# Two block scales rewritten as tensor_scalars, two convolution taps put beside a pair of state sums, and every slot chosen anew

## The chip, the core and the metric

The kernel runs on one core of a Trainium2 chip. A core has a matrix engine (TensorE, PE in the profile), a vector engine (VectorE, DVE), a scalar engine (ScalarE, ACT), a general engine (GpSimd, POOL), and SyncE (SP), which issues most of the DMAs here. Each engine takes its own instructions in order, and the engines wait for each other by semaphores. The metric is the device time of one execution in microseconds, lower is better. The kernel before takes 4279.77 us (median of 3 runs, 4276.45 to 4279.84).

## The reference

The input is x of shape (16, 1024, 256). Two blocks follow each other, both with a residual:

```
x = x + mamba(layernorm(x))
x = x + fp4_ffn(layernorm(x))

mamba:   xz = h @ in_proj.T;  x, z = split(xz)              # 512 channels each, 4 heads of 128
         x = silu(conv_b + sum_k xpad[:, k:k+L] * w[:, k])  # causal, 4 taps
         B, C, dt = per head projections of x (16 states)
         delta = softplus(dt @ dtw + dt_b)
         s = s * exp(delta * A) + (delta * x) * B           # for each of 16 states, over time
         y = (sum_n s_n * C_n + x * D) * silu(z);  out = y @ out_proj.T

fp4_quant_dequant(v): in blocks of 16 elements
         scale = max(max|v| / 6, 1e-12)
         q = nearest of (0, .5, 1, 1.5, 2, 3, 4, 6) to |v/scale|, with sign, times scale
ffn:     h = silu(q(v) @ q(w_gate).T) * (q(v) @ q(w_up).T);  out = q(h) @ q(w_down).T   # 256 -> 704 -> 256
```

## The kernel before

A *unit* is one head and one chunk of 512 time steps: 16 sequences, 2 chunks, 4 heads, so 128 units. There are also 128 *tiles* of 128 tokens for the normalisations and the feed-forward block, so one unit and one tile fall on the same stretch of time. A unit has 16 *steps*, one for each state n. In the second chunk of a sequence (a *late* unit) the scan starts from a carried value; in the first (an *early* unit) it starts from zero.

The scan runs on VectorE: in each step one `tensor_tensor_scan` over 512 columns (L990, tile `state`), and for twelve of the sixteen states also a product of the broadcast B row with delta*u in PSUM (L969, tile `db`). For the other four states GpSimd makes that product (`drive`, L739, tile `brow`). TensorE spreads a row of B over the partitions (`spread_b`, L1038), ScalarE makes exp(delta*A) (`decay_of`, L481). GpSimd multiplies two states at a time with C (`weigh`, L748, tile `prod`), and TensorE adds such a pair up (`sum_up`, L1053). It does that in quarters of its array: 64 rows by 64 columns each, the states of the pair into `ybank` and, crossed over, into `cross`. At the end `cross` is copied out, turned by `swap` and added to `ybank` (L1160), and VectorE multiplies with silu(z) (tile `yg`, L952).

Around the scan lie the jobs of the other stages. `timetable` gives each of them a slot: `due("post", 46)` is true in the step whose number is 46 modulo 16, in the unit that is 46 // 16 units behind the job's start. A job's slot number on an engine sets where it stands in that engine's order, and within a step the order of the `if` lines decides. On VectorE three places in a step take jobs: the product for the next step, `between`, the scan, and `behind`.

The jobs that the change and the prediction touch, with the lines of the profile:

- Block scales of the activations. VectorE takes the largest magnitude of each block of 16 (L831: 16 blocks of v in 256 columns, 44 blocks of h in 704 columns), then the scale (`block_scale`, L834), then its reciprocal (`block_recip`, L839). `block_scale` is a `scalar_tensor_tensor` with two inputs in SBUF: the maxima, and a one-column tile `least` that holds 1e-12, read again for each column. GpSimd then multiplies v (L803) or h (L780) by the reciprocals, and after the rounding by the scales (L788, L765).
- Rounding. ScalarE writes magnitudes to PSUM (L558 for v, L630 and L646 for the halves of h), VectorE adds and subtracts (`step_up`, L893, and `step_down`, L896). For h these are called `round_up_h` and `round_down_h`.
- The gate. TensorE makes the gate (L1108) and up (L1075) products in two halves of 352 columns, ScalarE the silu (L498), VectorE their product (`gated`, L903).
- The convolution. TensorE adds four taps into `pbank`: tap 0 in two diagonal quarters beside the D term (L1225, L1228), taps 1 to 3 as whole 128 by 128 products (`conv_tap`, L1061).
- delta. TensorE subtracts rounded pieces (L1281, L1168) and makes the dt product (L1156); ScalarE takes pieces (L580) and the softplus (L641) between two table loads (L638, L643).

All products in f32 come out as two instructions each in the trace.

## Time and profile before

| | |
|---|---|
| median of 3 runs | 4279.77 us |
| profiled execution | 4271.48 us |
| its span | 4269.6 us |
| busy: VectorE | 4170.9 us, 98% |
| busy: TensorE | 3979.2 us, 93% |
| busy: GpSimd | 3792.8 us, 89% |
| busy: ScalarE | 3697.7 us, 87% |
| first and last scan start | 87.7 and 4178.6 us |

Busy is the union of an engine's instructions over the span. On VectorE an instruction's record begins before the one ahead of it has ended, so what an instruction costs the engine is the distance from its start to the start of the next, some 0.07 to 0.1 us under its own duration. A short wait can hide in that overlap and does not show as idle time. Most of the span is one steady stretch in which units follow each other; in the first 90 us the weights are quantised, and in the last 90 us only the feed-forward of the last tiles is left.

### The profile page before, as it was taken

To read this page: it belongs to the slowest core of one execution; us is meant where nothing else is said; L and a number is where in the kernel's file an instruction comes from. 1 tells how busy PE (TensorE), PEld (TensorE's weight loads), DVE (VectorE), ACT (ScalarE), POOL (GpSimd) and SP (SyncE) were. 2 spreads that over 40 slices of the span, in tenths; PEclk is the share of its full clock that TensorE was granted. 3 is DMA by queue.
4 is the path that set the end of the run, shared out by engine and by line. 5 is a ranking of instruction groups with operands and counts; after the bars stand their busy time and mean duration, and the time that the engine had idled before them with its cause. 6 is when DMAs were issued, how large, how long until landed. Compare 5 with 4: busy or idle time off the path is not lost. (4 is left out here: it accounts for less than half of the span.)

```text
span 4269.6 us, 66216 instructions
## 1 busy us (share of the span) xinstructions
PE 3979.2 (93%) x19184; PEld 1930.0 (45%) x19500; DVE 4170.9 (98%) x5812; ACT 3697.7 (87%) x6808; POOL 3792.8 (89%) x2334
## 2 busy tenths in 40 slices
PE   4889999999999999999999999999999999999988
PEld 1234444444444444444444444444444444444445
DVE  6999999999999999999999999999999999999995
ACT  4889899898888889888888888989888888988874
POOL 5889999999999999999899999999999999999984
PEclk8999999999999999999999999999999999999999
DMA  3655555555555555555555555555555555555551
GB/s 98 199 178 184 176 177 182 178 177 181 179 175 181 181 172 183 179 172 181 176 174 181 181 175 178 183 177 177 180 180 176 178 182 172 182 180 174 180 172 33
DMA packets 288974, 739.16 MB, mean 173 GB/s; under 512 B 35686, under 2 KB 87014, under 8 KB 288614
## 3 DMA queue, kind: packets, MB, share of 16 engines
q1 hardware_dynamic: 286912, 732.75, 53.1%
q8 instruction: 159, 2.61, 0.2%
q10 hardware_dynamic: 1702, 2.16, 0.2%
q14 instruction: 201, 1.65, 0.1%
HBM read 709.61 MB, written 25.17 MB: 172 GB/s over the span
## 5 line engine op out<-in xcount | busy, mean ns | idle before, releaser
L748 POOL TENSOR_TENSOR prod<-state,cs 128x1024 f32<-128x1024 f32 x1024 | 2401.7, 2362 | 5.3 <-PE cross L1053 2.9
L1053 PE MATMUL ybank<-prod,ident 64*64 64x512 f32 x4096 | 997.0, 604 | 75.9 <-DVE state L990 55.7
L969 DVE TENSOR_TENSOR db<-db,du 128x512 f32<-128x512 f32 x1536 | 1046.2, 681 | 13.7 <-remote 7.3
L481 ACT ACTIVATE decay<-delta,aneg 128x512 f32<-128x512 f32 x1536 | 1029.4, 711 | 0.1
L1053 PE MATMUL cross<-prod,ident 64*64 64x512 f32 x4096 | 996.8, 605 | 0.0
L990 DVE TENSOR_TENSOR_SCAN state<-decay,carry,db 128x512 f32<-128x512 f32 x768 | 956.1, 1259 | 0.0
L990 DVE TENSOR_TENSOR_SCAN state<-decay,db 128x512 f32<-128x512 f32 x768 | 911.4, 1201 | 8.6 <-PE bank_b L1313 8.6
L739 POOL TENSOR_TENSOR brow<-brow,du 128x512 f32<-128x512 f32 x512 | 653.1, 1276 | 153.2 <-DMA brow<-b_rows 152.9
L1038 PE MATMUL db<-pieces,sel 128*128 128x512 bf16 x1220 | 468.0, 384 | 89.6 <-DVE state L990 88.4
L1053 PEld LDWEIGHTS ybank<-prod,ident 64*64 64x64 f32 x4096 | 239.8, 132 | 523.6 <-issue 386.6
L481 ACT ACTIVATE db<-delta,aneg 128x512 f32<-128x512 f32 x512 | 352.5, 688 | 137.3 <-DVE state L990 136.2
L1123 PE MATMUL bank_a<-wd,ht 128*128 128x256 f32 x1536 | 406.4, 389 | 4.3 <-ACT ht L506 1.2
L1038 PEld LDWEIGHTS db<-pieces,sel 128*128 128x128 bf16 x1536 | 149.4, 97 | 550.9 <-DVE state L990 354.2
L1123 PEld LDWEIGHTS bank_a<-wd,ht 128*128 128x128 f32 x1536 | 283.8, 191 | 205.2 <-issue 178.0
L1075 PE MATMUL bank_b<-wu,vt 128*128 128x352 f32 x1024 | 357.3, 471 | 0.0
L1108 PE MATMUL bank_a<-wg,vt 128*128 128x352 f32 x1024 | 347.5, 462 | 2.0 <-ACT hh L498 2.0
L990 DVE TENSOR_TENSOR_SCAN state<-db,carry,brow 128x512 f32<-128x512 f32 x256 | 325.5, 1272 | 0.0
L990 DVE TENSOR_TENSOR_SCAN state<-db,brow 128x512 f32<-128x512 f32 x256 | 310.1, 1211 | 0.0
L1075 PEld LDWEIGHTS bank_b<-wu,vt 128*128 128x128 f32 x1024 | 184.0, 189 | 215.5 <-issue 159.0
L1149 PE MATMUL pbank<-xnt,win 128*128 128x512 f32 x512 | 264.1, 601 | 2.3 <-ACT delta L641 1.8
L1138 PE MATMUL bank_a<-wo,yg 128*128 128x256 f32 x1024 | 265.2, 383 | 0.0
L1149 PE MATMUL bank_a<-xnt,win 128*128 128x512 f32 x512 | 262.5, 594 | 0.0
(140 smaller groups left out, 7240.6 us busy)
## 6 DMA issues: line engine op xcount, KB each, us to landing
cs<-c_rows SPq DMA_DIRECT2D x1024, 512.0 KB, 3.8
brow<-b_rows SPq DMA_DIRECT2D x512, 256.0 KB, 4.3
xin<-in_hidden SPq DMA_DIRECT2D x128, 128.0 KB, 4.5
xres<-in_hidden SPq DMA_DIRECT2D x128, 128.0 KB, 4.4
out_x<-ot SPq DMA_DIRECT2D x128, 128.0 KB, 3.4
c_rows<-xdbl SPq DMA_DIRECT2D x128, 32.0 KB, 2.1
b_rows<-xdbl SPq DMA_DIRECT2D x128, 32.0 KB, 2.0
win<-in_win_t SPq DMA_DIRECT2D x1, 1024.0 KB, 5.2
```

What stands on the lines that cost most here:

```text
L481: act.activation(out, delta[:, w.mod(2), :], ACT.Exp, scale=aneg[:, w.mod(HEADS), n:n + 1]).then_inc(done, 1)
L739: pool.tensor_tensor(brow[:, s, :], brow[:, s, :], du[:, w.mod(2), :], ALU.mult).then_inc(db_pool, 1)
L748: pool.tensor_tensor(prod[:, r, :, :], state[:, 2 * p:2 * p + 2, :], cs[:, c, :, :], ALU.mult).then_inc(weighted, 1)
L969: dve.tensor_tensor(t[:, :], t[:, :], du[:, gu % 2, :], ALU.mult).then_inc(db_done, 1)
L990: dve.tensor_tensor_scan(state[:, n, :], by, plus, start, ALU.mult, ALU.add).then_inc(scanned, 1)
L1038: pe.matmul(db[g % DB_BANKS][:, :], sel[:, gn, :], pieces[:, gu % 2, :], start=True, stop=True).then_inc(b_spread, 1)
L1053: last = pe.matmul((ybank, cross)[k][c * Q:(c + 1) * Q, :], ident[rows, rows], prod[rows, p % P_RING, k, :], start=(p == 0), stop=(k == 1 ...
L1075: last = pe.matmul(bank_b[:, 0:HALF], vt[:, k, :], wu[:, k, part * HALF:(part + 1) * HALF], start=(k == 0), stop=(k == KM - 1))
L1108: last = pe.matmul(bank_a[:, 0:HALF], vt[:, k, :], wg[:, k, part * HALF:(part + 1) * HALF], start=(k == 0), stop=(k == KM - 1))
L1123: last = pe.matmul(bank_a[:, 0:DM], ht[:, k, :], wd[:, k, :], start=(k == 0), stop=(k == KI - 1))
L1138: last = pe.matmul(bank_a[:, 0:DM], yg[:, t.mod(8) // 4, h, i * P:(i + 1) * P], wo[:, h, :], start=(h == 0), stop=(h == HEADS - 1))
L1149: return pe.matmul((pbank, bank_a)[part][:, :], win[:, k, part * DI + h * P:part * DI + (h + 1) * P], xnt[:, v.mod(8) // 4, k, :], start=( ...
```

## The change

1. `block_scale` is a `tensor_scalar` with two immediates (1/6 and 1e-12) in place of the `scalar_tensor_tensor`; the tile `least` is gone. For v, the maxima stand in a tile of their own and are read three times over (a dimension of step 0), and 48 columns are written in one run, of which the first 16 are used. For h, the maxima are written as 11 rows of 4 in a tile with 5 columns a row, and the scale reads these 11 rows of 4 and writes 44 columns in one run. The reciprocals move to other rows of the same tiles.
2. `taps_beside`: taps 1 and 2 of the convolution are computed as two diagonal quarters each (the matrix of a tap is diagonal, so the other two quarters are zero), and each quarter stands beside a crossed quarter of pair 1 of the state sums. Both states of pair 1 go into `cross`; `ybank` gets nothing of this pair. Tap 3 and the other seven pairs are as before.
3. All slots and the order of the `if` lines within a step are different on every engine, `between` is empty, and the buffer waits stay the same in kind.

```diff
-                return dve.scalar_tensor_tensor(s[:, 1, :], s[:, 0, :], 1.0 / 6.0,
-                                                least[0:s.shape[0], :].broadcast_to([s.shape[0], s.shape[2]]),
-                                                ALU.mult, ALU.max)
+                return dve.tensor_scalar(s[:, 1, :], s[:, 0, :], 1.0 / 6.0, SCALE_MIN, ALU.mult, ALU.max)
...
+            def v_scales():
+                three = v_max[:, None, :].broadcast_to([P, 3, DM // BLK])
+                return dve.tensor_scalar(vs[:, 0:3, :], three, 1.0 / 6.0, SCALE_MIN, ALU.mult, ALU.max)
+
+            def h_maxima(h):
+                return dve.tensor_reduce(h_max[:, :, 0:H_LONG], h.rearrange("p (a b k) -> p a b k", a=H_ROWS, k=BLK),
+                                         AX, ALU.max, apply_absolute_value=True)
+
+            def h_scales():
+                return dve.tensor_scalar(hs[:, 0, :].rearrange("p (a b) -> p a b", a=H_ROWS), h_max[:, :, 0:H_LONG],
+                                         1.0 / 6.0, SCALE_MIN, ALU.mult, ALU.max)
...
+            def taps_beside(v, w, p):
+
+                if v:
+                    x = xearly if v.mod(PER) < HEADS else xlate
+                if w:
+                    pe.wait_ge(weighted, w.val(PAIRS, p + 1))
+                for i in range(2):
+                    for r in range(2):
+                        rows, others = slice(r * Q, (r + 1) * Q), slice((1 - r) * Q, (2 - r) * Q)
+                        if v:
+                            pe.matmul(pbank[rows, :], cdiag[rows, v.mod(HEADS), i + 1, rows], x[rows, i + 1:i + 1 + CH],
+                                      start=False, stop=False, tile_position=(r * Q, r * Q), skip_group_check=True)
+                        if w:
+                            last = pe.matmul(cross[others, :], ident[rows, rows], prod[rows, p % P_RING, i, :],
+                                             start=False, stop=False, tile_position=(r * Q, (1 - r) * Q),
+                                             skip_group_check=True)
+                if w:
+                    last.then_inc(summed, 1)
...
-                if t := due("post", 36):
-                    gated(t, 0)
+                if t := due("post", 37):
+                    gated(t, 0)
```

Three places of the new order. First VectorE, in the middle of a late unit: the second half of a tile's quantisation work. `vs` and `hh` are the scales of v and the tile of h, `hw` the scratch of the rounding, `yg` the unit's gated output; a scan is listed as a SCALAR_TENSOR_TENSOR into `state`. Before:

```order
L903 TENSOR_TENSOR hh<-hh,bank_b 128x352
L969 TENSOR_TENSOR db<-db,du 128x512
L990 SCALAR_TENSOR_TENSOR state<-db,carry,brow 128x512
L893 SCALAR_TENSOR_TENSOR hw<-cross,hh 128x352
L831 TENSOR_REDUCE vs<-v_eps 128x16
L896 SCALAR_TENSOR_TENSOR hh<-cross,hw 128x352
L969 TENSOR_TENSOR db<-db,du 128x512
L990 SCALAR_TENSOR_TENSOR state<-decay,carry,db 128x512
L834 SCALAR_TENSOR_TENSOR vs<-vs,least 128x16
L952 TENSOR_TENSOR yg<-ybank,sz 128x512
L839 RECIPROCAL vs<-vs 128x16
L893 SCALAR_TENSOR_TENSOR hw<-cross,hh 128x352
```

Now the same work reads:

```order
L1004 SCALAR_TENSOR_TENSOR state<-db,carry,brow 128x512
L908 TENSOR_TENSOR hh<-hh,bank_b 128x352
L931 TENSOR_REDUCE v_max<-v_eps 128x16
L898 SCALAR_TENSOR_TENSOR hw<-cross,hh 128x352
L844 TENSOR_SCALAR vs<-v_max 128x48
L983 TENSOR_TENSOR db<-db,du 128x512
L1004 SCALAR_TENSOR_TENSOR state<-decay,carry,db 128x512
L901 SCALAR_TENSOR_TENSOR hh<-cross,hw 128x352
L921 RECIPROCAL vs<-vs 128x16
L983 TENSOR_TENSOR db<-db,du 128x512
L1004 SCALAR_TENSOR_TENSOR state<-decay,carry,db 128x512
L898 SCALAR_TENSOR_TENSOR hw<-cross,hh 128x352
```

The first `gated` (L903, now L908) moved behind the scan of the step whose `db` product used to follow it. The second rounding of h (the last row of each) moved behind one more product and scan, and `yg` moved from ahead of it to behind it.

Second TensorE, at the taps. `cdiag` holds the taps' diagonals, `win` the input projection, `sel` the selector for a row of B. Before:

```order
L1225 MATMUL pbank<-xearly,cdiag 64x512
L1228 MATMUL cross<-uu,ddiag 64x512
L1038 MATMUL db<-pieces,sel 128x512
L1149 MATMUL bank_a<-xnt,win 128x512
L1038 MATMUL db<-pieces,sel 128x512
L1237 MATMUL bank_b<-ident,v_eps 128x128 x2
L1061 MATMUL pbank<-xearly,cdiag 128x512 x3
L1149 MATMUL bank_a<-xnt,win 128x512
```

Now, from the last of the four rows of `taps_beside` on:

```order
L1090 MATMUL pbank<-xearly,cdiag 64x512
L1093 MATMUL cross<-prod,ident 64x512
L1067 MATMUL ybank<-prod,ident 64x512 x2
L1067 MATMUL cross<-prod,ident 64x512 x2
L1182 MATMUL bank_a<-xnt,win 128x512
L1052 MATMUL db<-pieces,sel 128x512
L1208 MATMUL bank_b<-ident,v_eps 128x128 x2
L1075 MATMUL pbank<-xearly,cdiag 128x512
L1052 MATMUL db<-pieces,sel 128x512
L1182 MATMUL bank_a<-xnt,win 128x512
```

The first two rows stand four times in a row in a unit; one whole tap is left of three, and pair 2 (the two rows at L1067) has come up to this place.

Third TensorE, around the up and gate products that ScalarE and VectorE wait for (`wu`, `wg`; `less` belongs to the pieces of B, `dtws` to delta, `swap` to the end of the sum). Before:

```order
L1075 MATMUL bank_b<-wu,vt 128x352 x2
L1038 MATMUL db<-pieces,sel 128x512
L1168 MATMUL pbank<-mid,less 128x512
L1108 MATMUL bank_a<-wg,vt 128x352 x2
L1038 MATMUL db<-pieces,sel 128x512
L1156 MATMUL pbank<-xdbl,dtws 128x512
L1160 MATMUL ybank<-xlate,swap 128x512
L1075 MATMUL bank_b<-wu,vt 128x352 x2
```

Now (up is L1108 here and gate L1141):

```order
L1052 MATMUL db<-pieces,sel 128x512
L1197 MATMUL pbank<-mid,less 128x512
L1108 MATMUL bank_b<-wu,vt 128x352 x2
L1141 MATMUL bank_a<-wg,vt 128x352 x2
L1052 MATMUL db<-pieces,sel 128x512
L1288 MATMUL pbank<-xdbl,dtws 128x512
L1052 MATMUL db<-pieces,sel 128x512
L1108 MATMUL bank_b<-wu,vt 128x352 x2
```

A selector product and the subtraction of pieces now stand ahead of the first up product; the product with `swap` moved behind the second one.

## Rows read from the trace of the kernel before

**Rows 1.** The page, part 1: busy us, share of the span, instructions.

```profile
PE 3979.2 (93%) x19184; PEld 1930.0 (45%) x19500; DVE 4170.9 (98%) x5812; ACT 3697.7 (87%) x6808; POOL 3792.8 (89%) x2334
```

**Rows 2.** Busy by stretch: stretch, its us; PE, PEld, DVE, ACT, POOL; clock, DMA, GB/s.

```profile
300.00:800.00 500.00, 476.18 (x2324) 231.06 (x2362) 499.23 (x703) 446.85 (x826) 456.81 (x282) 1.00 0.55 176
```

**Rows 3.** Waits of VectorE, whole span: us in total, times, longest.

```profile
DVE ot L939 <- PE bank_a L1123: 13.9, 8, 8.6
```

**Rows 4.** The same view, all there is between 500 and 4000 us.

```profile
DVE hh L903 <- PE bank_b L1075: 0.2, 1, 0.2
```

**Rows 5.** Line 834, the block scales: ns least/median/most, first and last start.

```profile
L834 DVE SCALAR_TENSOR_TENSOR vs<-vs,least x128: 141/160/744, 236.7 to 4237.0; 128x16 f32<-128x16 f32 x128
L834 DVE SCALAR_TENSOR_TENSOR hs<-hs,least x128: 189/389/2364, 282.4 to 4252.7; 128x44 f32<-128x44 f32 x128
```

**Rows 6.** Timeline of VectorE: start us, us, line, operation.

```profile
2020.08 2.33 DVE L834 SCALAR_TENSOR_TENSOR hs<-hs,least 128x44 f32<-128x44 f32 x1
2022.34 0.68 DVE L969 TENSOR_TENSOR db<-db,du 128x512 f32<-128x512 f32 x1
```

**Rows 7.** Timeline of GpSimd, the same stretch.

```profile
2020.00 2.36 POOL L748 TENSOR_TENSOR prod<-state,cs 128x1024 f32<-128x1024 f32 x1
```

**Rows 8.** Groups of VectorE instructions: busy us, mean ns of one, idle before.

```profile
L834 DVE SCALAR_TENSOR_TENSOR hs<-hs,least 128x44 f32<-128x44 f32 x128 | 57.2, 447 | 0.1
L834 DVE SCALAR_TENSOR_TENSOR vs<-vs,least 128x16 f32<-128x16 f32 x128 | 25.3, 198 | 0.0
L869 DVE SCALAR_TENSOR_TENSOR state<-state 88x2048 f32<-88x2048 f32 x2 | 4.5, 2253 | 0.0
L1010 DVE TENSOR_SCALAR cdiag<-ident,cw 128x128 f32<-128x128 f32 x16 | 3.5, 280 | 0.1
L846 DVE TENSOR_SCALAR state<-state 88x2048 f32<-88x2048 f32 x2 | 2.4, 1223 | 0.1
L1002 DVE TENSOR_SCALAR aneg<-aneg 128x64 f32<-128x64 f32 x1 | 0.2, 183 | 0.0
```

**Rows 9.** Timeline of VectorE in an early unit.

```profile
2126.18 2.32 DVE L990 TENSOR_TENSOR_SCAN state<-decay,db 128x512 f32<-128x512 f32 x2
2128.57 0.52 DVE L903 TENSOR_TENSOR hh<-hh,bank_b 128x352 f32<-128x352 f32 x1
2129.01 0.69 DVE L969 TENSOR_TENSOR db<-db,du 128x512 f32<-128x512 f32 x1
...
2132.51 1.21 DVE L990 TENSOR_TENSOR_SCAN state<-decay,db 128x512 f32<-128x512 f32 x1
2133.64 0.20 DVE L834 SCALAR_TENSOR_TENSOR vs<-vs,least 128x16 f32<-128x16 f32 x1
2133.76 0.68 DVE L952 TENSOR_TENSOR yg<-ybank,sz 128x512 f32<-128x512 f32 x1
2134.36 0.23 DVE L839 RECIPROCAL vs<-vs 128x16 f32<-128x16 f32 x1
2134.55 0.53 DVE L893 SCALAR_TENSOR_TENSOR hw<-cross,hh 128x352 f32<-128x352 bf16 x1
```

**Rows 10.** The same view in a late unit.

```profile
2037.86 0.24 DVE L839 RECIPROCAL vs<-vs 128x16 f32<-128x16 f32 x1
2038.01 0.48 DVE L893 SCALAR_TENSOR_TENSOR hw<-cross,hh 128x352 f32<-128x352 bf16 x1
```

**Rows 11.** Timeline of ScalarE in the early unit.

```profile
2134.05 0.47 ACT L646 ACTIVATE cross<-hh 128x352 f32<-128x352 f32 x1
```

**Rows 12.** Timeline of TensorE: the taps of a late unit, up in the early unit.

```profile
2009.14 0.60 PE L1225 MATMUL pbank<-xlate,cdiag 64*64 64x512 f32 x2
...
2009.57 0.59 PE L1225 MATMUL pbank<-xlate,cdiag 64*64 64x512 f32 x2
...
2011.63 2.74 PE L1061 MATMUL pbank<-xlate,cdiag 128*128 128x512 f32 x6
...
2127.08 1.45 PE L1075 MATMUL bank_b<-wu,vt 128*128 128x352 f32 x4
```

625 lines of the change are left out of this document (312 added, 313 removed).

## The prediction

> **What bounds the kernel now.** I read the engines' shares first: VectorE is busy for 98% of the span, TensorE 93%, GpSimd 89%, ScalarE 87% [rows 1]. A share is an average, so the busy time by stretch comes next: between 300 and 800 us VectorE is busy for 499.23 of 500 us, TensorE for 476.18, GpSimd for 456.81, ScalarE for 446.85 [rows 2]. Then the waits of VectorE: between 500 and 4000 us there is one, of 0.2 us [rows 4]; the long ones, such as 13.9 us for the down product, lie at the ends of the span [rows 3]. So in the steady stretch the time is the sum of what VectorE's instructions cost it, and what the other engines save counts only where VectorE waits for them. The last reading is therefore inside VectorE's busy time: which instructions take longer than their work? Two groups do.
>
> The block scales. That of h takes 189 ns at least, 389 in the median and 2364 at most, that of v 141, 160 and 744 [rows 5]. The work is the same each time, so the spread is waiting. One long one shows for what: it starts at 2020.08, lasts 2.33 us, and VectorE's next instruction starts at 2022.34 [rows 6], while GpSimd's product of 1024 columns runs from 2020.00 to 2022.36 [rows 7]. VectorE was held until GpSimd's instruction was over, and all that counts as busy. The Trainium skill ("SBUF — State Buffer", section "Who interferes with whom") says the same: VectorE and GpSimd share a pair of SBUF ports, one of them holds it for a whole instruction, and a VectorE instruction takes part with two SBUF inputs or in a two-port mode.
>
> Waits too short to show as idle. In an early unit the scan costs 1.13 us (2132.51 to 2133.64), but two scans ahead of `gated` take 2.39 (2126.18 to 2128.57) instead of 2.26 [rows 9]. The up product that `gated` needs starts at 2127.08 and is 1.45 long, so it ends at 2128.53 [rows 12]: 0.13 us are a wait. Likewise the reciprocal of v costs 0.19 us in the early unit (2134.36 to 2134.55) [rows 9] and 0.15 in a late one [rows 10], and the magnitudes that the instruction behind it needs end at 2134.52 [rows 11].
>
> **The change part by part.**
>
> The held time. For h the mean is 447 ns against 189 unhindered, for v 198 against 141 [rows 5, 8]. With 128 of each: 0.258 x 128 = 33.0 us and 0.057 x 128 = 7.3 us, together 40.3 us. It goes if the new tensor_scalar, which has one input in SBUF, doesn't need what GpSimd holds. The trace of before has no such instruction beside a busy GpSimd in the steady stretch, so the ends are 0 and 40.3; I take 40.3, because of the shapes. A contiguous tensor_scalar of 2048 columns takes 1223 ns, a scalar_tensor_tensor of as many 2253 [rows 8]: the first moves two columns in the time of one, which it can do only with a second way into SBUF. The change gives its tensor_scalars unlike outer counts (11 rows of 4 into one run of 44; 3 reads of 16 into one run of 48). The Trainium skill ("VectorE: DVE Perf Modes", section "What auto-detection actually checks") says that a one-source instruction takes two ports where the outermost counts of source and destination are both even or equal. By that rule 11 against 44 and 3 against 48 stay on one port, and no row of before can show it.
>
> The length of the new instructions. At one column a time, 2253 / 2048 = 1.1 ns a column [rows 8]. From the 141 ns of 16 columns [rows 5], 44 columns make 172 ns and 48 make 176. For h that is 17 ns less than 189, for v 35 ns more than 141: (35 - 17) x 128 = 2.3 us lost. The nearest rows bound it: 141 ns for both would be 6.1 us gained; 280 ns, the tensor_scalar of 128 columns with a scalar from memory, for both would be (91 + 139) x 128 = 29.4 us lost. The row nearest in size, 183 ns for 64 columns, speaks for the low end [rows 8]. The maxima of h keep their 704 columns in; only where 44 results go is new, and I cost it at nothing.
>
> The hidden waits. `gated` moves behind one product and one scan. A product of 512 columns is like `yg`, 0.60 us from start to start, and its own duration is the same (0.69 and 0.68) [rows 9]; with the scan that is 1.73 us. In front of the up product now stand a selector product and a piece of `less`, 0.4 us at most (the order shows them; on TensorE each is one instruction of 512 columns, and two of those in f32 cost 0.86 us by the taps below). So the up product has some 1.3 us to spare, and 0.13 x 64 early units = 8.3 us go. The second rounding of h gets a product and a scan more in front of it and loses `yg`: 1.13 us later against magnitudes that were just in time. 0.04 x 64 = 2.6 us go. The ends here are 0 and 10.9; I take 10.9, since both moves are far larger than the waits.
>
> The taps. Three whole taps take 2.74 us, 0.86 for one with the overlap at the end taken off; tap 0 in quarters beside the D term steps by 0.43 us twice, 0.86 as well [rows 12]. Two taps and a pair were 3 x 0.86 = 2.6 us and become 2 x 0.86 = 1.7: TensorE gains 0.86 us a unit, 110 us in all, and the time nothing, since TensorE isn't what ends last. If the quarters didn't run side by side, taps_beside would be 1.7 us longer, 0.86 more than before; TensorE's idle (23.8 in 500 us, 1.5 us a unit of 32 us [rows 2]) covers even that.
>
> The other slots. VectorE's instructions are as many and as long as before, whatever their order. GpSimd has 43 us of idle in 500, or 2.8 us a unit [rows 2], and its deadlines stand: the product of v by the reciprocals now comes behind a `drive`, with two scans more before its rounding is due. The copies of C and B keep three and two buffers, and each is still issued two or more steps ahead. In the last 90 us all depends on latencies through all engines; the chain of one tile has the same members, so I cost head and tail at nothing, with 8 us to either side (half of the longest wait group there, 13.9 [rows 3]).
>
> The sum: 40.3 - 2.3 + 10.9 = 48.9 us. From the profiled execution's 4271.5 us this gives 4222.6. The median of the runs is 8.3 us above the profiled execution, and I set the same saving against it: 4279.8 - 48.9 = 4230.9.
>
> **The rivals.**
>
> A. The tensor_scalars still wait for GpSimd and as long as before, so the change doesn't do what it says. For it: the fast contiguous tensor_scalar [rows 8]. Against: the unlike counts. The time: the hidden waits go, v is 4.5 us longer (0.035 x 128), 4279.8 - 10.9 + 4.5 = 4273.
>
> B. They wait, and in the new order they fall inside GpSimd's long products at random. Half of 2.36 us, times GpSimd's share of 0.89, for 256 instructions, is 269 us in place of 40.3 [rows 1, 7]; with the hidden waits gone, 4279.8 + 229 - 10.9 = 4498.
>
> C. A producer is late at a new place, and this is the case on the slow side. The place is the second rounding of h: it needs the magnitudes, which stand on ScalarE behind softplus and two table loads, behind the dt product, behind gate, behind the first up product. Before, that chain ended 0.03 us ahead of its user (2134.52 against 2134.55) [rows 9, 11], and every unit goes through it. For it: the chain has no slack today, and two small products moved in front of up. Against: 1.13 us more room, and TensorE is 0.86 us a unit shorter. It decides once the chain is 1.13 us longer than now against the scan; from 1.13 + 0.38 us on (48.9 / 128 = 0.38) the gain is eaten. One product's step beyond the room, 0.60 us, would be 77 us in 128 units: 4231 + 77 = 4308.
>
> D. The held time goes, but the hidden waits stay or turn up elsewhere, and the new instructions are nearer 280 ns: 4279.8 - 40.3 + up to 29.4, so 4240 to 4269, middle 4254.
>
> **How the numbers follow.** Forecast 0.74 (its own range 4221 to 4241), A 0.05, B 0.02, C 0.08, D 0.11. The low end is the forecast with the short instructions' 6 us more and some of the head's and tail's 8; the high end reaches to the middle of D: 4220 to 4256. Some 0.2 are left out. A measurement of this kernel can't tell less than about 0.2% (8.6 us) from no change. Faster by more: the forecast, most of D: 0.84. Within: A and the end of D: 0.06. Slower: B, C: 0.10.
>
> **What would show it.** In the profile after, the tensor_scalars of 44 and 48 columns should take 150 to 200 ns with hardly a spread; a longest one near 2 us shows A or B. VectorE should stay at 499 of 500 us in the steady stretch, with the same count of scans in less time: from the first to the last scan start 49 us less. The two early scans ahead of `gated` should cost 2.26 us, the reciprocal of v 0.15 in early units. TensorE's share should fall by 2 points. I am wrong if VectorE shows waits inside the steady stretch (the engine and line named there say where), or if the new instructions are long.

## The result and the profile after

The changed kernel takes 4287.26 us (median of 20 runs, 4279.98 to 4296.91) against 4278.77 us for the kernel before (20 runs). The ratio is 1.002, with a 95% interval of 1.0013 to 1.0026: slower by 0.2%. The forecast was 4231 us, so 56 us are missing. The profiled execution has a span of 4278.4 us, and the granted clock is 1.00 in the steady stretches as it was [rows 2].

The page's part 1 of the changed kernel, against [rows 1]:

```profile
PE 4017.5 (94%) x20012; PEld 1840.3 (43%) x20012; DVE 4130.5 (97%) x5812; ACT 3659.3 (86%) x6808; POOL 3795.3 (89%) x2333
```

VectorE is busy for 40 us less, as many instructions as before. Its work did get shorter; the time did not. The busy time by stretch, against [rows 2]:

```profile
300.00:800.00 500.00, 478.44 (x2405) 217.76 (x2403) 491.47 (x696) 439.20 (x819) 454.17 (x279) 1.00 0.54 176
```

VectorE is now idle for 8.5 of 500 us, where it had 0.8. The waits between 500 and 4000 us (who, for whom; us in total, times, longest) say where, against the single 0.2 us of [rows 4]:

```profile
POOL brow L741 <- DMA brow<-b_rows: 244.3, 204, 3.2
ACT v_eps L532 <- POOL ve L731: 104.4, 108, 1.5
DVE v_max L931 <- ACT v_eps L532: 44.0, 68, 1.1
```

VectorE waits for ScalarE's last scaling of v, ScalarE for GpSimd's reciprocal root, and GpSimd for the copy of a B row. In the kernel before the last of these waits read:

```profile
POOL brow L739 <- DMA brow<-b_rows: 126.0, 109, 1.6
```

The block scales themselves came out as forecast. Least, median and most of each in ns, against [rows 5]:

```profile
L844 DVE TENSOR_SCALAR vs<-v_max x128: 184/193/203, 237.1 to 4244.9; 128x48 f32<-128x48 f32 x128
L851 DVE TENSOR_SCALAR hs<-h_max x128: 167/173/200, 284.2 to 4261.1; 128x44 f32<-128x44 f32 x128
```

No spread is left. Added up from start to next start over the steady part, the scales of h cost VectorE 46.5 us before and 10.9 after, those of v 14.8 and 13.5: together 37 us less, for a forecast of 40.3 - 2.3 = 38.0. What took them back stands ahead of v's maxima: there the wait lies between the first `gated` and the reduction into `v_max`, and the steps of `gated` to the instruction behind it cost 162.0 us in all, where they cost 104.2 before. From the first to the last scan start it is 4101.0 us, where it was 4090.9: 32.04 us a unit for 31.96.

One unit of the changed kernel shows the chain. GpSimd, start and length (L750 is the product with C for a pair of states, L741 `drive`, L731 the root); the two earliest rows are one unit back:

```profile
1903.26 1.27 POOL L741 TENSOR_TENSOR brow<-brow,du 128x512 f32<-128x512 f32 x1 [1.66 <-DMA brow<-b_rows]
1904.49 2.37 POOL L750 TENSOR_TENSOR prod<-state,cs 128x1024 f32<-128x1024 f32 x1
...
1925.33 6.99 POOL L750 TENSOR_TENSOR prod<-state,cs 128x1024 f32<-128x1024 f32 x3
1932.28 1.26 POOL L741 TENSOR_TENSOR brow<-brow,du 128x512 f32<-128x512 f32 x1
1935.87 1.27 POOL L741 TENSOR_TENSOR brow<-brow,du 128x512 f32<-128x512 f32 x1 [2.32 <-DMA brow<-b_rows]
1937.10 2.36 POOL L750 TENSOR_TENSOR prod<-state,cs 128x1024 f32<-128x1024 f32 x1
1939.41 1.39 POOL L776 TENSOR_TENSOR hh<-hh,hs 128x704 f32<-128x704 f32 x1
1940.76 2.35 POOL L750 TENSOR_TENSOR prod<-state,cs 128x1024 f32<-128x1024 f32 x1
1943.08 0.68 POOL L731 TENSOR_TENSOR ve<-ve,minus_half 128x2 f32<-128x2 f32 x1
```

SyncE's queue (start and length of each issue; L392 is `spread_c`, L404 `copy_b`):

```profile
1930.07 0.32 SPq L392 DMA_DIRECT2D cs<-c_rows  x1
1930.44 0.43 SPq L404 DMA_DIRECT2D brow<-b_rows  x1
```

ScalarE, then VectorE:

```profile
1943.79 0.51 ACT L532 ACTIVATE v_eps<-v_eps,ve 128x256 f32<-128x256 f32 x1 [1.53 <-POOL ve L731]
```

```profile
1942.70 0.50 DVE L908 TENSOR_TENSOR hh<-hh,bank_b 128x352 f32<-128x352 f32 x1
1944.33 0.42 DVE L931 TENSOR_REDUCE v_max<-v_eps 128x16 f32<-128x256 f32 x1 [1.14 <-ACT v_eps L532]
```

The three products in one row are those for pairs 4, 5 and 6 (a pair n holds the states 2n and 2n + 1). The copies of C have three buffers, so the next unit's first one waits for pair 5, which ends at 1925.33 + 2/3 x 6.99 = 1929.99. SyncE issues it at 1930.07, and the copy of B row 5, which had a free buffer (the scan of state 13 that read it had started at 1928.25, 1.21 long), stands behind it in the queue: issued at 1930.44. GpSimd can start `drive` for state 5 only at 1935.87, and everything behind it on GpSimd waits too: pair 7, the scaling of h, pair 0, the root. And the chain closes on itself, because the next pair 5 stands behind all of those. From `drive` 5 at 1903.26 to the end of pair 5 are 26.7 us, to the issue 0.5, to the next `drive` 5 at 1935.87 another 5.4: 32.6 us. That sum is the length of this unit, however it is cut; what makes it a loop is that each part waits for the one ahead of it, and that VectorE alone would need less (31.5, below). It is the same in all of the stretch: over the 109 units between 500 and 4000 us the three parts are 26.9, 0.4 and 4.9 us in the mean, and `drive` 5 waits for its copy in every one of them, 1.3 us at least. Of the 26.9 us GpSimd waits 1.1, for other B rows and for VectorE's scales and rounding of v. The experiments test whether this loop sets the time.

In the kernel before, B row 5 was copied ahead of this C copy, and `drive` 5 stood behind pair 7. On SyncE the lines are these:

```diff
-                if w := due("scan", 0):
-                    spread_c(w, 0)
...
-                if w := due("scan", -3):
-                    copy_b(w, 5)
...
+                if w := due("scan", -2):
+                    spread_c(w, 0)
+                if w := due("scan", -2):
+                    copy_b(w, 5)
```

### The profile page after: what moved, and what is told of

Read it like the earlier page. It is cut to its first block and busy times, and to the rows that moved or that the text cites. A ratio compares the mean times of both kernels' runs of the same rounds, so it can differ in the third digit from the quotient of the medians.

```text
span 4278.4 us, 67554 instructions
## 1 busy us (share of the span) xinstructions
PE 4017.5 (94%) x20012; PEld 1840.3 (43%) x20012; DVE 4130.5 (97%) x5812; ACT 3659.3 (86%) x6808; POOL 3795.3 (89%) x2333
## 5 line engine op out<-in xcount | busy, mean ns | idle before, releaser
L750 POOL TENSOR_TENSOR prod<-state,cs 128x1024 f32<-128x1024 f32 x1024 | 2406.4, 2362 | 14.1 <-DVE state L1004 14.1
L484 ACT ACTIVATE decay<-delta,aneg 128x512 f32<-128x512 f32 x1536 | 1061.6, 713 | 117.9 <-DVE state L1004 117.7
L1067 PE MATMUL ybank<-prod,ident 64*64 64x512 f32 x3584 | 917.8, 608 | 21.7 <-POOL prod L750 16.1
L1067 PE MATMUL cross<-prod,ident 64*64 64x512 f32 x3584 | 917.7, 608 | 0.0
L741 POOL TENSOR_TENSOR brow<-brow,du 128x512 f32<-128x512 f32 x512 | 652.0, 1274 | 295.9 <-DMA brow<-b_rows 290.3
L1052 PE MATMUL db<-pieces,sel 128*128 128x512 bf16 x1536 | 592.4, 386 | 151.5 <-DVE state L1004 129.6
L1067 PEld LDWEIGHTS ybank<-prod,ident 64*64 64x64 f32 x3584 | 203.2, 132 | 454.9 <-issue 223.1
L1156 PE MATMUL bank_a<-wd,ht 128*128 128x256 f32 x1536 | 393.0, 380 | 1.2 <-ACT ht L509 1.2
L1156 PEld LDWEIGHTS bank_a<-wd,ht 128*128 128x128 f32 x1536 | 292.6, 191 | 195.9 <-issue 171.2
L1141 PE MATMUL bank_a<-wg,vt 128*128 128x352 f32 x1024 | 345.3, 460 | 2.9 <-ACT hh L501 2.0
L1108 PE MATMUL bank_b<-wu,vt 128*128 128x352 f32 x1024 | 344.9, 459 | 0.0
L1182 PE MATMUL bank_a<-xnt,win 128*128 128x512 f32 x512 | 274.6, 618 | 0.0
L1093 PE MATMUL cross<-prod,ident 64*64 64x512 f32 x1024 | 248.4, 602 | 0.0
L1108 PEld LDWEIGHTS bank_b<-wu,vt 128*128 128x128 f32 x1024 | 194.4, 190 | 118.4 <-issue 40.9
```

The lines of the kernel that those rows point to most:

```text
L484: act.activation(out, delta[:, w.mod(2), :], ACT.Exp, scale=aneg[:, w.mod(HEADS), n:n + 1]).then_inc(done, 1)
L741: pool.tensor_tensor(brow[:, s, :], brow[:, s, :], du[:, w.mod(2), :], ALU.mult).then_inc(db_pool, 1)
L750: pool.tensor_tensor(prod[:, r, :, :], state[:, 2 * p:2 * p + 2, :], cs[:, c, :, :], ALU.mult).then_inc(weighted, 1)
L1052: pe.matmul(db[g % DB_BANKS][:, :], sel[:, gn, :], pieces[:, gu % 2, :], start=True, stop=True).then_inc(b_spread, 1)
L1067: last = pe.matmul((ybank, cross)[k][c * Q:(c + 1) * Q, :], ident[rows, rows], prod[rows, p % P_RING, k, :], start=(p == 0), stop=(k == 1 ...
L1093: last = pe.matmul(cross[others, :], ident[rows, rows], prod[rows, p % P_RING, i, :], start=False, stop=False, tile_position=(r * Q, (1 - ...
```

## The experiments

Each ratio is to the kernel before on the same chip, with its 95% interval. The runs are from several chips, so a difference of medians between two numbers can be off by some us; a length from the first to the last scan start is that of one execution. In the expectations, "the product for state n" on GpSimd is the product for pair n.

**1. The root first.** The first theory (P) took only GpSimd's order at the root: pair 0 stands ahead of it.

```diff
-                if w := due("scan", 3):
-                    weigh(w, 0)
                 t1, t2 = due("norm", 3), due("post", 19)
                 if t1 or t2:
                     rstd(t1, t2)
+                if w := due("scan", 3):
+                    weigh(w, 0)
```

> The changed kernel, with GpSimd's reciprocal root (rstd) put ahead of the first product of the step with C (weigh 0), as it was before the change. Theory P (GpSimd's order): the largest magnitudes of v wait for ScalarE, and ScalarE for this root, which comes 2.36 us earlier; the some 58 us that VectorE loses there (0.43 us in 122 units and more) all go: 4287 - 55 = 4232 us, ratio 0.989, and the wait on L532 is gone. Rival Q (the chain is as late through TensorE and ScalarE, the pieces and the copy of cross stand right in front of it): less than 15 us go, 4272 to 4287. Rival R: VectorE then waits at another place of the new order, 4250 to 4270, and the waits name it.

Measured: 4309.11 us (4307.17 to 4316.78), ratio 1.0065 [1.0053, 1.0078]. The theory fell: the kernel got slower, outside the times of both rivals too, though a wait at another place is what rival R named. VectorE's wait for v's maxima is gone, and another took its place. The waits between 500 and 4000 us:

```profile
POOL brow L741 <- DMA brow<-b_rows: 332.7, 224, 3.4
DVE db L983 <- PE db L1052: 58.5, 73, 2.9
```

TensorE waited for pair 7, with a selector product behind it that VectorE needs:

```profile
1982.08 0.65 PE L1067 MATMUL ybank<-prod,ident 64*64 64x512 f32 x2 [1.80 <-POOL prod L750]
...
1983.11 0.39 PE L1052 MATMUL db<-pieces,sel 128*128 128x512 bf16 x1
1983.33 0.38 PE L1197 MATMUL pbank<-mid,less 128*128 128x512 bf16 x1
1983.55 1.35 PE L1108 MATMUL bank_b<-wu,vt 128*128 128x352 f32 x4
```

GpSimd's wait for the B row grew by 88 us. The wait at v's maxima was thus only the place where a late GpSimd showed; the cause had to lie ahead of pair 7, at the copy. What the 22 us themselves are is only half known: from `drive` 5 to the end of pair 5 it takes no longer than in the changed kernel (26.8 us in the mean of its units for 26.9), but from the copy's issue to `drive` 5 it takes 5.2 us for 4.9, and no run shows why.

**2. The scales alone, in the old slots.**

```diff
-                return dve.scalar_tensor_tensor(s[:, 1, :], s[:, 0, :], 1.0 / 6.0,
-                                                least[0:s.shape[0], :].broadcast_to([s.shape[0], s.shape[2]]),
-                                                ALU.mult, ALU.max)
+                three = v_max[:, None, :].broadcast_to([P, 3, DM // BLK])
+                return dve.tensor_scalar(vs[:, 0:3, :], three, 1.0 / 6.0, SCALE_MIN, ALU.mult, ALU.max)
...
+                return dve.tensor_scalar(hs[:, 0, :].rearrange("p (a b) -> p a b", a=H_ROWS), h_max[:, :, 0:H_LONG],
+                                         1.0 / 6.0, SCALE_MIN, ALU.mult, ALU.max)
```

> The kernel before with the new block scales alone; slots and taps as before. Theory P: the held time of 40.3 us goes and the longer scale of v costs some 6, and the short waits ahead of gated and the second rounding take back up to 7 us, since they hang on chains that are no faster: 4279 - 30 = 4249 us (4243 to 4252), ratio 0.993. Rival S: held time is only moved, since GpSimd or TensorE is as full as VectorE: 4272 to 4281.

Measured: 4272.3 us, ratio 0.9975 [0.9966, 0.9984]. That is 11 us, and most of the gain is missing; in the profiled execution the distance from the first to the last scan is no shorter at all (4093.9 us for 4090.9, 31.98 a unit). VectorE is busy for 494 of 500 us, and has this wait between 500 and 4000 us, where the kernel before has 0.2 us:

```profile
DVE hh L919 <- PE bank_b L1092: 34.0, 71, 1.1
```

So even with the old slots the shorter VectorE ran into something that takes 32.0 us a unit. The time is the one that rival S gave (4272 to 4281), but it isn't that GpSimd or TensorE is full. Theory P had priced the waits ahead of `gated` at 7 us at most. Number 12 comes back to it.

**3. The old scales in the new slots.**

```diff
-                three = v_max[:, None, :].broadcast_to([P, 3, DM // BLK])
-                return dve.tensor_scalar(vs[:, 0:3, :], three, 1.0 / 6.0, SCALE_MIN, ALU.mult, ALU.max)
+                return dve.scalar_tensor_tensor(vs[:, 0, :], v_max[:, :], 1.0 / 6.0,
+                                                least[:, :].broadcast_to([P, DM // BLK]), ALU.mult, ALU.max)
...
-                return dve.tensor_scalar(hs[:, 0, :].rearrange("p (a b) -> p a b", a=H_ROWS), h_max[:, :, 0:H_LONG],
-                                         1.0 / 6.0, SCALE_MIN, ALU.mult, ALU.max)
+                return dve.scalar_tensor_tensor(hs[:, 0, :], h_flat, 1.0 / 6.0,
+                                                least[:, :].broadcast_to([P, INNER // BLK]), ALU.mult, ALU.max)
```

> The changed kernel with block scales of two SBUF inputs, as before the change; slots and taps as changed. Theory P: in the new order they fall within GpSimd's products of 2.36 us, so they are held longer than the mean 0.26 and 0.06 us of before; the scale of h starts 1.2 us ahead of the end of such a product, that of v some 0.5 to 1: some 1.2 x 128 = 150 us for h and up to 100 for v, less up to 58 where that hides the wait for v: 4380 to 4480. Rival T: they are held as much as before, 40 us: 4320.

Measured: 4418.6 us, ratio 1.0316 [1.0302, 1.033]. In the new order the two-input form falls inside GpSimd's products nearly every time:

```profile
L854 DVE SCALAR_TENSOR_TENSOR hs<-h_max,least x128: 203/982/1297, 286.9 to 4395.3; 128x44 f32<-128x44 f32 x128
L846 DVE SCALAR_TENSOR_TENSOR vs<-v_max,least x128: 157/802/1316, 237.9 to 4379.0; 128x16 f32<-128x16 f32 x128
```

The means are 1078 and 721 ns:

```profile
L854 DVE SCALAR_TENSOR_TENSOR hs<-h_max,least 128x44 f32<-128x44 f32 x128 | 138.0, 1078 | 0.2
L846 DVE SCALAR_TENSOR_TENSOR vs<-v_max,least 128x16 f32<-128x16 f32 x128 | 92.3, 721 | 0.1
```

The scales and the slots belong together: in these slots the new scales are worth 131 us (4418.6 - 4287.3), in the old ones 11. They were held for longer than 131 us (188, below), but the wait for v's maxima shrinks beside it, from 44.0 to 10.0 us between 500 and 4000 us.

**4. The copy of B row 5 first.** The changed kernel, with two `if`s of SyncE's queue exchanged.

```diff
-                if w := due("scan", -2):
-                    spread_c(w, 0)
                 if w := due("scan", -2):
                     copy_b(w, 5)
+                if w := due("scan", -2):
+                    spread_c(w, 0)
```

> The changed kernel with SyncE's copy of B row 5 ahead of the copy of the first C rows (same slot). Theory P: GpSimd's product for state 5 waits up to 2.3 us for this copy, which stands behind a copy that waits for GpSimd; it starts 0.4 to 1.0 us earlier, and with it the root. Of VectorE's 0.45 us a unit most goes: 4287 - 40 = 4247 (4240 to 4262). Rival U: the copy isn't earlier or the wait isn't on this path: 4280 to 4290.

Measured: 4208.35 us (4206.73 to 4211.31), ratio 0.9825 [0.9812, 0.9839]. 79 us for two lines. SyncE and GpSimd in one unit, to be held against the rows of the changed kernel:

```profile
1954.92 0.32 SPq L404 DMA_DIRECT2D brow<-b_rows  x1
1955.50 7.73 SPq L392 DMA_DIRECT2D cs<-c_rows  x3
```

```profile
1957.69 1.29 POOL L741 TENSOR_TENSOR brow<-brow,du 128x512 f32<-128x512 f32 x1
1959.29 1.27 POOL L741 TENSOR_TENSOR brow<-brow,du 128x512 f32<-128x512 f32 x1 [0.31 <-DMA brow<-b_rows]
```

The copy reaches GpSimd 4.4 us after its issue (1954.92 to 1959.29) and the wait is 0.31 us in place of 2.32. VectorE's waits between 500 and 4000 us are one of 0.2 us, and it fills the stretch:

```profile
300.00:800.00 500.00, 486.48 (x2463) 227.35 (x2463) 500.00 (x709) 448.64 (x839) 463.33 (x285) 1.00 0.57 181
```

From the first to the last scan start it is 4028.0 us, 31.47 a unit: that is VectorE's own length. The expectation had the sign and the place right and missed the size by half: 79 us, or 73 from the first to the last scan start, for 40. It took the steps of `gated` ahead of v's maxima to lose most of their 58 us, and they lost all of it (162.0 us before the exchange, 103.7 after); the other 15 us lie in pieces of 4.5 us and less in front of scans and products.

**5. Like outer counts.** Number 4 with the scales as tensor_scalars of 44 columns into 44, and 16 into 16.

```diff
-                three = v_max[:, None, :].broadcast_to([P, 3, DM // BLK])
-                return dve.tensor_scalar(vs[:, 0:3, :], three, 1.0 / 6.0, SCALE_MIN, ALU.mult, ALU.max)
+                return dve.tensor_scalar(vs[:, 0, :], v_max[:, :], 1.0 / 6.0, SCALE_MIN, ALU.mult, ALU.max)
...
-                return dve.tensor_scalar(hs[:, 0, :].rearrange("p (a b) -> p a b", a=H_ROWS), h_max[:, :, 0:H_LONG],
-                                         1.0 / 6.0, SCALE_MIN, ALU.mult, ALU.max)
+                return dve.tensor_scalar(hs[:, 0, :], h_flat, 1.0 / 6.0, SCALE_MIN, ALU.mult, ALU.max)
```

> The changed kernel with the copy of B row 5 first (as in e4_copy_first, 4208 us), and both block scales as tensor_scalars with like outer counts: 44 columns in one run to 44, 16 to 16. Theory P (the unlike counts keep the instruction on one port): these two are held by GpSimd's products again; in these slots the two-input form was held for a mean of 0.9 us (h) and 0.55 us (v) each, so 4208 + 130 to 185 = 4340 to 4390 us, ratio 1.015 to 1.025. Rival V (one input is enough to be free, whatever the counts): 4200 to 4212, a bit faster than e4 since v has 16 columns in place of 48.

Measured: 4354.82 us, ratio 1.0185 [1.0171, 1.0198]. Held again:

```profile
L851 DVE TENSOR_SCALAR hs<-h_max x128: 186/958/1274, 279.8 to 4341.6; 128x44 f32<-128x44 f32 x128
L844 DVE TENSOR_SCALAR vs<-v_max x128: 154/382/1261, 233.2 to 4323.9; 128x16 f32<-128x16 f32 x128
```

By groups (busy us, mean ns of one, idle before), and under it the same of the changed kernel:

```profile
L851 DVE TENSOR_SCALAR hs<-h_max 128x44 f32<-128x44 f32 x128 | 135.1, 1055 | 0.2
L844 DVE TENSOR_SCALAR vs<-v_max 128x16 f32<-128x16 f32 x128 | 61.7, 482 | 0.1
```

```profile
L844 DVE TENSOR_SCALAR vs<-v_max 128x48 f32<-128x48 f32 x128 | 24.7, 193 | 0.1
L851 DVE TENSOR_SCALAR hs<-h_max 128x44 f32<-128x44 f32 x128 | 22.3, 174 | 0.2
```

(0.881 + 0.289) x 128 = 150 us more, and 146 were measured against number 4. One input is not enough; the form of the operands decides. The Trainium skill ("VectorE: DVE Perf Modes", section "What auto-detection actually checks") says that a one-source instruction takes both ports where the outermost counts of source and destination are both even or equal: 44 and 44, 16 and 16 here, against 11 and 44, 3 and 48 in the changed kernel. Both halves of that rule agree with the rows. They don't single it out: the two free forms also read several rows and the two held ones a single run, and no run has like counts with a source in rows.

**6. The taps beside pair 1, in the old slots.** Number 2 with `taps_beside`.

```diff
-                if v := due("pre", 10):
-                    conv_tap(v, 1)
-                if v := due("pre", 10):
-                    conv_tap(v, 2)
+                v, w = due("pre", 10), due("scan", 10)
+                taps_beside(v, w, 1)
...
-                if w := due("scan", 8):
-                    sum_up(w, (1,))
```

> The kernel before with the new block scales (as in e2_scales_only, ratio 0.9975) and with two taps beside pair 1; all slots as before, pair 1 moves from step 8 to step 10. Theory P: in the old slots VectorE's gain is turned into waits ahead of gated on the first up product, which hangs on a chain from a scan on (three pairs, up), and the 0.86 us that TensorE saves lies elsewhere: no gain over e2, ratio 0.996 to 0.9985. Rival W: TensorE as a whole is full there (487 of 500 us) and its load is what makes it late: the saving goes to the time, ratio 0.989 to 0.992.

Measured: 4267.63 us, ratio 0.9976 [0.9967, 0.9984], that of number 2. The time gets nothing. TensorE's busy time between 300 and 800 us falls from 486.51 to 476.17, but that says little of the taps: with all taps whole the kernel before had 476.18 [rows 2], and number 2, with the same products in the same order, 486.51.

**7. Whole taps in the fast kernel.** Number 4 with taps 1 and 2 whole again.

```diff
-                v, w = due("pre", 10), due("scan", 10)
-                taps_beside(v, w, 1)
+                if v := due("pre", 10):
+                    conv_tap(v, 1)
+                if v := due("pre", 10):
+                    conv_tap(v, 2)
+                if w := due("scan", 10):
+                    sum_up(w, (1,))
```

> The changed kernel with the copy of B row 5 first, and taps 1 and 2 whole again, pair 1 in its own quarters behind them. TensorE has 0.86 us more to do in each unit of 31.5 us, and was busy for 487 of 500 us: that makes it just full. Theory P: some of it shows, 0.1 to 0.5 us a unit: 4208 + 15 to 60 = 4223 to 4270. Rival X: what TensorE has to do there isn't ahead of anything that VectorE waits for: 4205 to 4213.

Measured: 4210.38 us, ratio 0.9846 [0.9833, 0.986]; the medians of 7 and 4 lie 2 us apart, on two chips, and from the first to the last scan start it is 4028.7 us for 4028.0. Here too the quarters give nothing that can be told, though they do save TensorE what the forecast said. Here two whole taps and pair 1 take 2.71 us, from 2011.69 to the start of pair 2 at 2014.40, and in number 4 the `taps_beside` 1.77, from 2011.53 to 2013.30.

```profile
2011.69 1.88 PE L1075 MATMUL pbank<-xlate,cdiag 128*128 128x512 f32 x4
...
2014.40 0.60 PE L1067 MATMUL ybank<-prod,ident 64*64 64x512 f32 x2
```

```profile
2011.53 0.64 PE L1090 MATMUL pbank<-xlate,cdiag 64*64 64x512 f32 x1
...
2013.30 0.59 PE L1067 MATMUL ybank<-prod,ident 64*64 64x512 f32 x1
```

**8. Drive 5 behind pair 7.** The other edge of the loop: SyncE as in the changed kernel, `drive` 5 on GpSimd where it stood before.

```diff
-                if w := due("scan", 0):
-                    drive(w, 5)
                 if w := due("scan", 16):
                     weigh(w, 7)
+                if w := due("scan", 0):
+                    drive(w, 5)
```

> The changed kernel with GpSimd's product for state 5 put behind weigh 7 instead of ahead of it, as it was before the change; SyncE's order is the changed one. Theory P (a closed loop: weigh 5, copy of B row 5, product for state 5, and all of GpSimd's other work back to weigh 5): weigh 7's 2.35 us now lie beside the copy's 5.4, GpSimd's wait of 2.3 us goes to under 0.3, and the time is that of e4: 4205 to 4220. Rival Y: the copy's place in SyncE's queue is itself what costs: 4260 to 4290.

Measured: 4205.51 us (4204.59 to 4207.46), ratio 0.9836 [0.9823, 0.985]. The copy is as late as in the changed kernel, and it no longer matters, since 2.4 us of other work stand ahead of its user. Between 500 and 4000 us:

```profile
POOL brow L741 <- DMA brow<-b_rows: 8.5, 18, 0.8
```

It takes both edits, the late copy and the early `drive`, to make the loop.

**9. Both edits of order, and a shorter scale of v.** The edits of numbers 4 and 8, and for v 9 rows of 2 (with a pitch of 3) into a run of 18, in place of 48.

```diff
-                three = v_max[:, None, :].broadcast_to([P, 3, DM // BLK])
-                return dve.tensor_scalar(vs[:, 0:3, :], three, 1.0 / 6.0, SCALE_MIN, ALU.mult, ALU.max)
+                return dve.tensor_scalar(vs[:, :].rearrange("p (a b) -> p a b", a=9), v_max[:, :, 0:2],
+                                         1.0 / 6.0, SCALE_MIN, ALU.mult, ALU.max)
```

> Edit: the changed kernel with the copy of B row 5 ahead of the copies of C on SyncE, the drive for state 5 behind the product for state 7 on GpSimd, and v's scale written over 18 columns of a run instead of 48. Theory (the loop of copy and GpSimd work is open, VectorE alone bounds): the two edits of order gave 4208 and 4206 us each alone and have nothing left to add to each other; the shorter scale gives about 30 ns in each of 128 steps, 4 us, so 4200 to 4206 us, ratio .981 to .983. Rival (something else than VectorE's own length now ends the unit, such as TensorE at 486 of 500 us): the shorter scale gives nothing, 4206 to 4210 us. Second rival: the two moves disturb each other, 4215 us or more.

Measured: 4203.09 us (4199.84 to 4203.32), ratio 0.9819 [0.9806, 0.9833]: the fastest of all. From the first to the last scan start it takes 4022.3 us, number 8 takes 4026.1: 3.8 us less, where 4 were expected. VectorE shows no wait between 500 and 4000 us. The interval overlaps those of 4 and 8, so the 4 us rest on the traces: the steps of v's scale cost VectorE 9.6 us there and 13.5 in number 8.

**10. The root first, with the copy first.** The edits of numbers 1 and 4, as they stand there.

```diff
                 if w := due("scan", -2):
+                    copy_b(w, 5)
+                if w := due("scan", -2):
                     spread_c(w, 0)
-                if w := due("scan", -2):
-                    copy_b(w, 5)
...
-                if w := due("scan", 3):
-                    weigh(w, 0)
                 t1, t2 = due("norm", 3), due("post", 19)
                 if t1 or t2:
                     rstd(t1, t2)
+                if w := due("scan", 3):
+                    weigh(w, 0)
```

> Edit: the changed kernel with both the reciprocal root ahead of the product for state 0 on GpSimd (alone it gave 4309 us) and the copy of B row 5 ahead of the copies of C on SyncE (alone 4208 us). Loop theory (the root first lost because it lengthened a loop that was already the longest, copy of row 5, drive 5, product 7 and the rest of GpSimd's unit, product 5): with the copy early the loop has slack, the loss goes, 4203 to 4215 us, ratio about .983. Rival (root first costs by itself, since the products behind it end later for TensorE): its 22 us stay, 4228 to 4235 us.

Measured: 4205.73 us (4205.04 to 4206.22), ratio 0.9827 [0.9814, 0.9841]. The 22 us that number 1 lost are nothing once the copy is early. That the root had lengthened the loop, as the expectation says, is not what the trace of number 1 shows (above): moving it changes no work in the loop.

**11. The copy later still.** The changed kernel, with the copy of row 5 behind the next C copy as well, which waits for pair 6.

```diff
                 if w := due("scan", 0):
                     spread_c(w, 1)
+                if w := due("scan", 0):
+                    copy_b(w, 5)
...
-                if w := due("scan", -2):
-                    copy_b(w, 5)
```

> Edit: the changed kernel with the copy of B row 5 one place later still on SyncE, behind the next copies of C, which wait for the product for state 6. Loop theory: the copy starts one more GpSimd product later (2.35 us, and 0.4 us for the issue), and the unit is as long as the loop, so each of the 128 units grows by 2.0 to 2.75 us: 256 to 352 us on 4287, so 4540 to 4640 us, ratio 1.06 to 1.085; GpSimd's wait for brow grows by about as much. Rival (the copy's place is on the path only at times, and the loss is the late root's own): 4285 to 4310 us.

Measured: 4556.27 us (4551.97 to 4561.39), ratio 1.0647 [1.0633, 1.0662]: 269 us more than the changed kernel, 2.1 us a unit, for a copy that is issued one GpSimd product (2.3 us) later. SyncE and GpSimd:

```profile
2017.45 2.59 SPq L392 DMA_DIRECT2D cs<-c_rows  x2
2020.09 0.43 SPq L404 DMA_DIRECT2D brow<-b_rows  x1
```

```profile
2025.13 1.27 POOL L741 TENSOR_TENSOR brow<-brow,du 128x512 f32<-128x512 f32 x1 [4.20 <-DMA brow<-b_rows]
```

The unit follows the copy nearly one to one, which a wait beside a bound engine would not do.

**12. Scales alone, copy of row 1 first.** Number 2, with one copy moved on SyncE.

```diff
+                if w := due("scan", -4):
+                    copy_b(w, 1)
                 if w := due("scan", 12):
                     spread_c(w, 6)
...
-                if w := due("scan", -3):
-                    copy_b(w, 1)
```

> Edit: the kernel before with the new block scales alone (that gave 4272 us), and on SyncE the copy of B row 1 ahead of the C copy that waits for the product for state 3, one place earlier. Theory (before had the same loop, only slack enough: product 3, copy of row 1, drive 1 with 1.3 us of idle ahead of it, the products up to 7, pair 7 on TensorE, up product, and the first gated on VectorE; when the scales stop holding VectorE, this loop ends the unit at 32.0 us): with the copy earlier the held time shows as forecast, 38 us off the kernel before, and some or all of the hidden waits stay, since gated stands where it stood: 4232 to 4248 us, ratio .989 to .992, and the waits for the up product all but vanish. Rival (TensorE, 486 of 500 us with the whole taps, sets the unit): nothing changes, 4268 to 4276 us, ratio .997 to .999.

Measured: 4230.99 us (4229.01 to 4235.11), ratio 0.9893 [0.9876, 0.9909], 41 us below number 2, and 43 us less from the first to the last scan start (4051.0). The theory's range ended at 4232. GpSimd has no wait for a B row left between 500 and 4000 us. The wait for the up product between 500 and 4000 us, and the stretch:

```profile
DVE hh L919 <- PE bank_b L1092: 0.8, 2, 0.5
```

```profile
300.00:800.00 500.00, 482.51 (x2343) 234.31 (x2381) 498.94 (x705) 452.14 (x833) 461.49 (x282) 1.00 0.57 180
```

The kernel before had the same kind of loop at another place: pair 3, the C copy that waits for it, the copy of row 1 behind that, `drive` 1. Here it is in number 2, 32.0 us a unit. In the first row the second copy of C is the one that waits, and in the second row the first copy of B is that of row 1. VectorE waits further down the line, and GpSimd in turn for VectorE's reciprocals of v. So this loop doesn't close over GpSimd's work alone, but runs by TensorE's up product and VectorE's `gated`:

```profile
1975.12 6.61 SPq L393 DMA_DIRECT2D cs<-c_rows  x2
1981.83 3.44 SPq L405 DMA_DIRECT2D brow<-b_rows  x2
```

```profile
1986.25 1.27 POOL L743 TENSOR_TENSOR brow<-brow,du 128x512 f32<-128x512 f32 x1 [1.32 <-DMA brow<-b_rows]
...
2003.25 0.62 POOL L807 TENSOR_TENSOR v_eps<-v_eps,vs 128x256 f32<-128x256 f32 x1 [0.92 <-DVE vs L973]
```

```profile
1997.05 0.52 DVE L919 TENSOR_TENSOR hh<-hh,bank_b 128x352 f32<-128x352 f32 x1 [0.38 <-PE bank_b L1092]
```

With VectorE at 31.96 us a unit before, the loop did not show on VectorE. It stood right behind it: GpSimd's wait for row 1 is there in the kernel before too, 109 times between 500 and 4000 us, once in each unit.

## Why the prediction was wrong

**"VectorE's busy time is what counts": true of the kernel before, and only just.** Number 2 shows that a second bound lay close behind: of the 38 us of the scales 11 came through. The reading of [rows 2], GpSimd 43 us idle in 500 and so with 2.8 us of room a unit, took idle time for room. Between 500 and 4000 us GpSimd was idle for 308 us. 126 of them were the wait for the B row, once a unit, inside such a loop, and the other 182 waits for VectorE. I had not looked at what GpSimd's idle time was made of.

**The held time and the length of the new instructions: right.** 37 us for 38.0. The instructions take 167 to 203 ns without spread; the least rows of 141 ns and the 280 ns of the far bound were both off, the 183 ns of the nearest size was close. Numbers 3 and 5 show from two sides what would have happened with two inputs or like counts. Rival A is out. Rival B's mechanism is real, but for the forms that the change does not use: in number 3 the means are 1078 and 721 ns against 189 and 141 unhindered, (0.889 + 0.580) x 128 = 188 us held, for the 269 of a fall at random.

**The hidden waits: right in kind, mis-sized.** They were put at 10.9 us. The first is a wait: in the early units of the kernel before `gated` starts 0.04 us behind the end of the up product, and in number 4 0.7 us or more behind it. (The room ahead of the up product was worked out loosely: the forecast's own 0.43 us for each of two products makes 0.86, not 0.4; in the rows of number 1 they take 0.44, from 1983.11 to 1983.55.) In number 4 the distance from first to last scan is 62.8 us less than before, 37 of it the scales; the other 26 us lie in steps where the profile of before shows no idle time. The steps from the scans of early units on give 11.9 us (8.3 forecast), the reciprocals of v 4.6 (2.6 forecast), and the rest lies in pieces below 5 us each, of which no run shows how much is waiting. So with the loop open the kernel takes 4208 us and passes the low end of the range, 4220. Number 12 keeps the old slots and most of these waits, and its distance is 39.9 us less.

**The taps: right.** Numbers 6 and 7: TensorE is spared 0.94 us a unit (0.86 forecast), and the time gets nothing. The page of the changed kernel has TensorE at 94% instead of 2 points less, so that sign failed as a sign. Its busy share doesn't measure its load here: it differs by 10 us in 500 with the same products in the same order (the kernel before and number 2), and by 8 among numbers 4, 8, 9 and 10, which have the same products too.

**"The copies of C and B keep three and two buffers, and each is still issued two or more steps ahead": the step that failed.** Counted in steps, it holds for row 5. In time it does not, since SyncE's queue is in order and the C copy in front waits for GpSimd's pair 5. And "GpSimd has 43 us of idle in 500 and its deadlines stand" failed with it: `drive` 5 had moved ahead of pair 7. Numbers 4 and 8 undo one half each and give 79 and 82 us; number 11 makes it worse by 2.1 us a unit; numbers 1 and 10 show that the wait seen on VectorE is a symptom. The forecast put this term at nothing; it cost 73 us from the first to the last scan start (number 4). The forecast looked at the engines' order on VectorE and TensorE and took SyncE's from its slot numbers.

**Rival C** (a late producer at a new place) is what happened, with the right sign and at another place: not the magnitudes of h behind two small products, but v's maxima behind the copy. Its price was worked out for one place only; had it been the loop, the sum would have been worked out from GpSimd and SyncE: 26.7 + 0.5 + 5.4 = 32.6 us in the unit shown, and 32.04 in the mean of all.

So the change holds three parts, here by the length from the first to the last scan start. The scales are worth 40 us once the loop of the old slots is open (number 12), 37 of them in their own steps, and their length no longer hangs on what GpSimd does. The new slots with the taps are worth another 23 to 25 (numbers 4 and 8 against 12). And in these slots the late copy on SyncE and the early `drive` on GpSimd together cost 73 to 75, or 79 to 82 in the medians. The fastest version is 1.8% below the kernel before.

What stays open: why the copy of row 5 takes longer in one unit than in another. Behind a C copy of 512 KB issued just ahead it took 5.4 us to its use (1930.44 to 1935.87) and 4.8 one unit earlier, ahead of it 4.4 (number 4), 5.0 in number 11. From issue to landing it is 4.8 us in the mean in the changed kernel and 4.1 in number 4. No run separates the copy's own time from its company.

## What to carry to other kernels

When the bound engine gets shorter, look for the loop right behind it: an engine's idle time that is made of one repeated wait is part of a period, not room, so follow that wait once round and add up its length per iteration. Give every DMA queue an order by when each entry can start: a copy whose buffer is free must not stand behind one that waits for compute. And if removing a wait on the bound engine makes it slower, the wait was where the delay showed, and its source is further up.

## What the runs showed of the hardware

- A tensor_scalar with one input in SBUF was held beside GpSimd's products by 0.9 us in the mean when it read one run of 44 columns and wrote one (1055 ns for 186 at least), and not at all when it read 11 rows of 4 and wrote a run of 44 (174 ns for 167 at least), with the same GpSimd work. Whether the unlike counts or the rows do it, no run tells.
- The same two-input instruction took 447 ns in the mean in one order [rows 8] and 1078 in another: the price of what it shares with GpSimd is set by where it falls, so such an instruction makes an order brittle.
- The copies of a B row (256 KB each) landed 3.4 to 6.2 us after their issue in the changed kernel, 4.4 in the median of the 434 between 500 and 4000 us, so one that is issued two steps of 2 us ahead of its user is mostly late.
